# Expert tiles as 32-column strips turned by VectorE instead of TensorE, and landing numbers read before they are needed

## The reference

```
x = layernorm(x + memory_layer(x))        # projections, short convolution, cumulative sums of cos and sin features
flat = x.reshape(4096, 128)
probs = softmax(flat @ router_w.T)        # 8 experts
topk_p, topk_i = top_k(probs, 2); weights = topk_p / sum(topk_p)
out = sum over experts e of square(relu(flat @ w_fc[e].T)) @ w_proj[e].T * combine[:, e]   # w_fc[e]: 512 x 128
out += square(relu(flat @ shared_fc.T)) @ shared_proj.T
x = layernorm(x + out)
```

## Time and profile before

| | us |
|---|---|
| median of 3 runs (lowest, highest) | 480.66 (480.43, 483.86) |
| the profiled execution | 480.25 |
| its span in the profile | 478.4 |
| TensorE busy | 443.9 (93%) |
| VectorE busy | 356.6 (75%) |
| ScalarE busy | 354.9 (74%) |
| GpSimd busy | 318.1 (66%) |

### The profile page before, as it was taken

One profiled execution on the slowest core, in us unless ns is written; L12 is line 12 of the kernel. 1 busy time (PEld: TensorE's weight loads), 2 busy tenths in 40 slices (PEclk: granted clock), 3 DMA queues, 4 the chain that ended last, 5 costly groups with the idle time before them and its releaser, 6 DMA issues.

```text
span 478.4 us, 7874 instructions
## 1 busy us (share of the span) xinstructions
PE 443.9 (93%) x2193; PEld 288.9 (60%) x2193; DVE 356.6 (75%) x870; ACT 354.9 (74%) x557; POOL 318.1 (66%) x294
## 2 busy tenths in 40 slices
PE   8997999999999998877889988999999999999973
PEld 5343444444344333334666766789999999999821
DVE  5889999999999999999888977453333333555465
ACT  3989999999999999952675555556666666666655
POOL 4763788888898989881677667734555545655541
PEclk9998999999999999999999999999999999999999
DMA  8032226673434343200111111142223221222457
GB/s 284 11 93 84 78 73 214 217 245 136 157 136 159 136 157 136 92 1 1 47 45 52 50 41 52 55 111 59 69 68 85 67 65 53 62 70 66 147 176 220
DMA packets 41196, 48.68 MB, mean 102 GB/s; under 512 B 5616, under 2 KB 25266, under 8 KB 41152
## 3 DMA queue, kind: packets, MB, share of 16 engines
q1 hardware_dynamic: 35792, 39.16, 25.0%
q0 software_dynamic: 5216, 8.70, 6.0%
q10 hardware_dynamic: 144, 0.31, 0.3%
HBM read 19.26 MB, written 29.11 MB: 101 GB/s over the span
## 4 chain that ended last, share of the span: by engine, by line
PE 43%; POOL 22%; DVE 17%; issue 8%; ACT 6%; SPq 2%; DMA 2%; POOLq 0%; DVEq 0%; ACTq 0%
POOL memory_feat L505 17%; PE routed_ph L1591 13%; PE routed_po L1606 13%; PE dispatch_spo L1074 3%; PE dispatch_sph L1064 3%; DVE memory_y_raw L788 2%; POOL memory_feat L513 2%; DVE memory_prod L779 2%; POOL memory_prod L528 2%; PE routed_px L1579 2%; PE memory_nsum L630 2%; SPq L1737 1%; DVE memory_feat L779 1%; PE memory_ph L636 1%; DVE dispatch_stats L1319 1%
## 5 line engine op out<-in xcount | busy, mean ns | idle before, releaser
L505 POOL TENSOR_TENSOR memory_feat<-memory_feat,memory_p_tok 128x1024 f32<-128x1024 f32 x64 | 125.9, 2063 | 17.1 <-ACT memory_feat L400 14.2
L630 PE MATMUL memory_nsum<-memory_feat,tri 128*128 128x512 f32 x256 | 116.8, 598 | 6.3 <-ACT memory_last_rows L413 2.4
L1567 POOL DMA_INDIRECT pick_scratch<-routed_ob,routed_xg x71 | 72.1, 1016 | 65.2 <-DVE routed_ob L1689 52.0
L630 PEld LDWEIGHTS memory_nsum<-memory_feat,tri 128*128 128x128 f32 x256 | 47.6, 191 | 64.4 <-issue 54.6
L1274 POOL DMA_INDIRECT table_scratch<-dispatch_xrow,dispatch_slot x64 | 62.3, 973 | 30.3 <-issue 14.4
L1639 ACT ACTIVATE routed_rel<-routed_ph 128x512 f32<-128x512 f32 x71 | 42.3, 597 | 45.0 <-PE routed_ph L1591 45.0
L1689 DVE TENSOR_SCALAR routed_ob<-routed_po,routed_xg 128x128 f32<-128x128 f32 x71 | 22.6, 348 | 67.2 <-PE routed_po L1606 67.1
L1606 PE MATMUL routed_po<-routed_w2c,routed_hid 128*128 128x128 f32 x568 | 71.1, 275 | 0.5 <-ACT routed_hid L1648 0.5
L1591 PE MATMUL routed_ph<-routed_xs,routed_w1c 128*128 128x256 f32 (+1 forms) x368 | 71.2, 337 | 0.0
L779 DVE TENSOR_TENSOR memory_prod<-memory_nsum,memory_query 128x1024 f32<-128x1024 f32 x58 | 68.8, 1216 | 2.0 <-PE memory_nsum L630 1.8
L1606 PEld LDWEIGHTS routed_po<-routed_w2c,routed_hid 128*128 128x128 f32 x568 | 67.0, 192 | 0.8 <-ACT routed_hid L1648 0.7
(11 more groups left out here) (202 smaller groups left out, 695.6 us busy)
## 6 DMA issues: line engine op xcount, KB each, us to landing
table_scratch<-memory_blank SPq DMA_DIRECT2D x68, 260.0 KB, 2.6
dispatch_xrow<-pick_scratch SPq DMA_DIRECT2D x16, 256.0 KB, 3.1
routed_xg<-table_scratch SPq DMA_DIRECT2D x25, 130.0 KB, 2.2
w<-w_up SPq DMA_DIRECT2D x9, 256.0 KB, 2.7
w<-w_down SPq DMA_DIRECT2D x9, 256.0 KB, 3.2
x_tok<-x SPq DMA_DIRECT2D x4, 512.0 KB, 3.7
out<-x_tok SPq DMA_DIRECT2D x7, 256.0 KB, 4.1
routed_xg<-table_scratch SPq DMA_DIRECT2D x21, 65.0 KB, 1.9
```

Of the source, the lines that this page charges most:

```text
L505: nc.gpsimd.tensor_tensor(v, v, pv, ALU.mult).then_inc(wfeat_done, 1)
L630: last = nc.tensor.matmul(nsum[:, o:o + 512], tri[:], feat[:, i % U, h, q * 512:(q + 1) * 512], start=True, stop=True)
L1567: nc.gpsimd.indirect_dma_start(out=pick_dram, in_=ob[:, u, h, :], in_offset=None, out_offset=bass.IndirectOffsetOnAxis(ap=xg[:, t % XU, h, ...
```

## The change

It is made of four edits.

1. A full tile is no longer loaded as 256 rows but as four strips of 32 columns each. A strip goes to 32 partitions of `xb`, cut into 32 x 32 blocks: one DMA with 256 runs of 128 bytes. The two words at the end of each row (place and weight) go to `mark` with a fifth DMA. Tiles 0 and 1 have all four strips begun by SyncE; from tile 2 on SyncE begins two and ScalarE two. Half tiles are loaded as before, into an `xg` that now has one slot of 128 rows for each tile.
2. VectorE turns the 32 x 32 blocks with one instruction for a full tile, from `xb` to `xs`. TensorE's transposes and ScalarE's copies stay for half tiles alone.
3. ScalarE waits at its start of the stage until all 8 groups are in the table, so that it need not know `needs`. Tile 2 is begun ahead of its first relu, then two tiles in each of the steps 0, 1 and 2 (tiles 3 to 8), then tile t+6 in step t, always behind the squares.
4. The numbers of `settle` are read by SyncE in tiles 10 to 17, one group in each, and kept in registers. The two loads of a group now share a semaphore.

```diff
@@ build
-            rou.sync(sp)
-            fin.sync(sp)
+            due = rou.sync(sp)
+            fin.sync(sp, due)
@@ routed
+    ASK_AT = 10
+    SQ = 32
+    STRIPS = D // SQ
+    ALONE = 2
+    LEAD = 6
-        xg = sb("xg", [P, XU, HALVES, RW])
+        xb = sb("xb", [P, XU, ROWS])
+        mark = sb("mark", [P, XU, HALVES, RW - D])
+        xg = sb("xg", [P, XU, RW])
...
+        def by_sync(t):
+            return STRIPS if t < ALONE else STRIPS // 2
...
+        def strip(t, j, rows):
+            return (xb[j * SQ:(j + 1) * SQ, t % XU, :].rearrange("a (i b) -> a i b", b=SQ),
+                    rows[:, j * SQ:(j + 1) * SQ].rearrange("(i a) b -> a i b", a=SQ))
...
+            def full(t):
+                first = sp.value_load(start[0:1, t:t + 1], min_val=0, max_val=TABLE - ROWS)
+                groups = sp.value_load(needs[0:1, t:t + 1], min_val=1, max_val=NG)
+                rows = table[bass.ds(first, ROWS), :]
+                sp.wait_ge(dis.grouped, groups)
+                if not early(t, XU):
+                    sp.wait_ge(blocked, t - XU + 1)
+                for j in range(by_sync(t)):
+                    to, of = strip(t, j, rows)
+                    sp.dma_start(to, of).then_inc(stripped[t % XU], 16)
+                if not early(t, XU):
+                    sp.wait_ge(scattered[t % U], passes(t - XU))
+                sp.dma_start(mark[:, t % XU], rows[:, D:].rearrange("(h p) c -> p h c", p=P)).then_inc(loaded[t % XU], 16)
...
+            def body(t, u):
+                load(t, u)
+                g = t - ASK_AT
+                if g == 0:
+                    sp.wait_ge(dis.settled, 1)
+                if 0 <= g < NG:
+                    due.append([sp.value_load(settle[g:g + 1, n:n + 1], min_val=16, max_val=32 * TILES) for n in range(U)])
...
         def tensor(pe):
             def up(t, u):
-                pe.wait_ge(x_kept, t + 1)
+                if t < FULL:
+                    pe.wait_ge(blocked, t + 1)
+                else:
+                    pe.wait_ge(x_kept, t - FULL + 1)
...
             def front():
-                turn(0, 0)
-                turn(1, 1)
                 up(0, 0)
...
-                if not beyond(t, 2):
-                    turn(t + 2, (u + 2) % U)
+                if not beyond(t, 2) and t + 2 >= FULL:
+                    turn(t + 2)
...
         def scalar(act):
+            def load(t):
+                first = act.value_load(start[0:1, t:t + 1], min_val=0, max_val=TABLE - ROWS)
+                if not early(t, XU):
+                    act.wait_ge(blocked, t - XU + 1)
+                rows = table[bass.ds(first, ROWS), :]
+                for j in range(by_sync(t), STRIPS):
+                    to, of = strip(t, j, rows)
+                    act.dma_start(to, of).then_inc(stripped[t % XU], 16)
+
+            def begun(t):
+                return min(FULL, 2 * t + 5, t + LEAD + 1)
...
             def front():
-                keep_x(0, 0)
-                keep_x(1, 1)
+                act.wait_ge(dis.grouped, NG)
+                for t in range(ALONE, begun(-1)):
+                    load(t)
                 rectified(0, 0)
                 squared(0, 0)
...
                 if not beyond(t, 1):
                     squared(t + 1, (u + 1) % U)
+                for n in range(begun(t - 1), begun(t)):
+                    load(n)
...
         def vector(dve):
+            def turn(t):
+                dve.wait_ge(stripped[t % XU], 16 * STRIPS * (t // XU + 1))
+                if not early(t, 2):
+                    dve.wait_ge(up_done, parts(t - 1))
+                nc.vector.transpose(xs[:, t % 2, :], xb[:, t % XU, :]).then_inc(blocked, 1)
+
+            def front():
+                turn(0)
+                turn(1)
+
             def body(t, u):
                 if not beyond(t, 3):
                     weights(dve, t + 3, (u + 3) % U)
+                if t + 2 < FULL:
+                    turn(t + 2)
                 dve.wait_ge(down_done, t + 1)
+                dve.wait_ge(loaded[t % XU], 16 * (t // XU + 1))
@@ finish
-        def sync(sp):
-            sp.wait_ge(dis.settled, 1)
-
+        def sync(sp, due):
             def load(g):
-                due = [sp.value_load(settle[g:g + 1, u:u + 1], min_val=16, max_val=32 * TILES) for u in range(U)]
                 for u in range(U):
-                    sp.wait_ge(rou.scattered[u], due[u])
+                    sp.wait_ge(rou.scattered[u], due[g][u])
```

More of the change, by code:

```diff
@@ L98, in build @@
         late = Late(nc, c, early.xrow, x_tok)
-        rou = routed(nc, c, dis, ident, w1, w2, expert, start, needs, table, pick_dram)
-        fin = finish(nc, c, late, dis, rou, ident, y_all, eps, warm, settle, pick_dram, out)
+        rou = routed(nc, c, dis, ident, w1, w2, expert, start, needs, settle, table, pick_dram)
+        fin = finish(nc, c, late, rou, ident, y_all, eps, warm, pick_dram, out)
         block = c.enter_context(nc.Block())
@@ L1480, in dispatch, with routed @@
                              grouped=grouped, tabled=tabled, experts_in=experts_in, added=added, settled=settled)
-def routed(nc, outer, dis, ident, w1, w2, expert, start, needs, table, pick_dram):
+def routed(nc, outer, dis, ident, w1, w2, expert, start, needs, settle, table, pick_dram):
     HALVES = ROWS // P
@@ L1508, in routed @@
         px = ps("px", [P, FC * P])
+        stripped = [sem(f"stripped{u}") for u in range(XU)]
         loaded = [sem(f"loaded{u}") for u in range(XU)]
+        blocked = sem("blocked")
         scattered = [sem(f"scattered{u}") for u in range(U)]
@@ L1550, in load @@
                 first = sp.value_load(start[0:1, t:t + 1], min_val=0, max_val=TABLE - ROWS)
[L1551 to L1561 removed]
+                if t == FULL:
+                    sp.wait_ge(dis.grouped, NG)
+                sp.wait_ge(scattered[t % U], passes(t - XU))
+                sp.dma_start(xg[:, row_of(t)], table[bass.ds(first, P), :]).then_inc(loaded[row_of(t)], 16)
+            def load(t, u):
+                if t < FULL:
+                    full(t)
+                else:
+                    half(t)
+            due = []
+            def body(t, u):
[5 more added lines that the diff above has]
+                    due.append([sp.value_load(settle[g:g + 1, n:n + 1], min_val=16, max_val=32 * TILES) for n in range(U)])
+            tiles(lambda: None, body)
+            return due
         def gpsimd(pool):
@@ L1565, in body @@
                 pool.wait_ge(kept, t + 1)
-                for h in range(height(t)):
+                for h, own in enumerate(marks(t)):
                     nc.gpsimd.indirect_dma_start(
                         out=pick_dram, in_=ob[:, u, h, :], in_offset=None,
-                        out_offset=bass.IndirectOffsetOnAxis(ap=xg[:, t % XU, h, D:D + 1].bitcast(U32), axis=0),
+                        out_offset=bass.IndirectOffsetOnAxis(ap=own[:, 0:1].bitcast(U32), axis=0),
                         bounds_check=2 * NTOK - 1, oob_is_err=False).then_inc(scattered[u], 16)
@@ L1573, in tensor @@
         def tensor(pe):
-            def turn(t, u):
-                pe.wait_ge(loaded[t % XU], 16 * (t // XU) + 16)
-                if not early(t, 1):
-                    pe.wait_ge(x_kept, t)
-                for h in range(height(t)):
-                    last = nc.tensor.transpose(px[:, h * P:(h + 1) * P], xg[:, t % XU, h, 0:D], ident[:])
-                last.then_inc(turned, 1)
+            def turn(t):
+                pe.wait_ge(loaded[row_of(t)], 16 * (t // XU) + 16)
+                if t > FULL:
+                    pe.wait_ge(x_kept, t - FULL)
+                nc.tensor.transpose(px[:, 0:P], xg[:, row_of(t), 0:D], ident[:]).then_inc(turned, 1)
             def up(t, u):
                 s = u % 2
-                pe.wait_ge(x_kept, t + 1)
+                if t < FULL:
+                    pe.wait_ge(blocked, t + 1)
+                else:
+                    pe.wait_ge(x_kept, t - FULL + 1)
                 pe.wait_ge(w_ready, t + 1)
@@ L1712, in finish @@
         both = [c.enter_context(nc.psum_tensor(f"finish_both{g}", [P, GT * D], F32)) for g in range(NG)]
-        picked = [[sem(f"picked{g}_{r}") for r in range(2)] for g in range(NG)]
+        picked = [sem(f"picked{g}") for g in range(NG)]
         both_done = sem("both_done")
@@ L1822, in gpsimd @@
             for n, g in enumerate(BY_POOL):
-                for r in range(2):
-                    pool.wait_ge(picked[g][r], 16)
+                pool.wait_ge(picked[g], 32)
                 v = slice(g * GT, (g + 1) * GT)
@@ L1831, in add_up @@
             def add_up():
-                for r in range(2):
-                    dve.wait_ge(picked[0][r], 16)
+                dve.wait_ge(picked[0], 32)
                 v = slice(0, GT)
```

49 lines of the change are left out of this document (21 added, 28 removed).

## The result

The changed kernel takes 483.28 us (median of 20 runs, 481.63 to 486.08) beside 480.64 us for the kernel before (20 runs, 479.11 to 485.23). The ratio is 1.0044, 95% interval 1.0027 to 1.0061: slower by 2.1 us by the ratio (the two medians lie 2.6 us apart), which is inside the 1% called "within". The forecast was 475.2 us, faster by 5.5. The profiled execution took 484.4 us with a span of 482.6, that is 1.1 us over its median and 4.2 us over the profiled one before.

What follows compares the result with a forecast made beforehand. TensorE was taken to bound full and half tiles, SyncE's register reads the end. The terms -4.9 + 1.9 + 0.5 - 3.0 = -5.5 us took 480.66 to 475.2; own range 472.5 to 477, overall 472.0 to 481.0.

Steps and rivals of the forecast that it cites:

- SyncE's lag: Tiles 10 to 17: SyncE falls 11 us behind against a 13 us lead; charged at nothing, upper end 2 us.
- the last stage: End: with early reads, ScalarE and VectorE set about 1.95 us a group; -3.0 us, ends -1 and -4.5.
- transposes off TensorE: Full tiles: 23 steps lose 0.215 us each once TensorE no longer transposes; -4.9 us.
- start of up(0): First up of the full tiles waits for VectorE's first turn, beginning near 318.8; +1.9 us.
- rival B: Start: TensorE's 3.0 us pause drops the granted clock to 0.50, costing 1.7 us, 476.9 in all; chance 0.10.
- ScalarE issuing: Steps 0 to 2, two tiles each: ScalarE 1.1 us over, slack absorbing most; +0.5 us, ends 0 and 1.5.
- rival C: Full steps: ScalarE's issuing doesn't overlap its squares, a tile costs 4.2 us against 3.52; slower, 489.5; chance 0.13.
- rule of overlap: Full tiles: ScalarE's issuing runs beside its squares, as VectorE's register read did; 2.9 us a tile instead of 4.2.
- DMA engines: Full tiles: at 34 ns a piece, 2.7 us plus 0.4 of scatters fit inside 3.52; engines bound from 39 ns.
- rival D: Full tiles: short runs choke the DMA engines; at 45 ns each, 4.0 us a tile, 486.7, slower; chance 0.06.
- rival E: Last stage: ScalarE's best pace, some 1.75 us a group, 0.8 us more gain, 473.8 in all; chance 0.08.
- rival A: Last stage: SyncE's reads didn't pace it; real pace 2.5 us a group, gain there 0.8, 477.4; chance 0.13.

Runs made afterwards that it cites:

- after: The changed kernel, with all four edits made to the kernel before: 483.28 us, ratio 1.0044 to the kernel before.
- no_pool: The changed kernel with GpSimd's adds for groups 2 to 6 given to TensorE: 481.6 us, ratio 1.0014 to the kernel before.
- reads_spread: The changed kernel with SyncE's 32 reads of settle one to a tile, tiles 9 to 40: 480.97 us, ratio 0.9998 to the kernel before.
- shift_ts: The changed kernel with each shift made by four tensor_scalar instead of one scalar_tensor_tensor: 480.61 us, ratio 0.9987 to the kernel before.
- spread_ts3: The changed kernel with reads one to a tile and the first three shifts by four tensor_scalar each: 476.33 us, ratio 0.9896 to the kernel before.
- reads_back: The changed kernel with the reads of settle back in the last stage, strips kept: 479.97 us, ratio 0.9978 to the kernel before.
- warm: The changed kernel with 7 unused 128x512 matmuls ahead of the first up: 482.63 us, ratio 1.0019 to the kernel before.
- warm3: The changed kernel with 3 unused 128x512 matmuls ahead of the first up: 484.25 us, ratio 1.0072 to the kernel before.
- turns_first: The changed kernel with earlier turns of tiles 0 and 1, SyncE alone loading three tiles, ScalarE's wait behind its first squares: 484.57 us, ratio 1.0094.
- spread_turns: The changed kernel with reads one to a tile plus the edit of turns_first: 476.42 us, ratio 0.9907 to the kernel before.
- spread_turns_ts3: The changed kernel with spread reads, the edit of turns_first and the first three shifts by tensor_scalar: 473.26 us, ratio 0.9830 to the kernel before.
- reads_alone: The kernel before with only the reads of settle moved to tiles 10 to 17, no strips: 481.95 us, ratio 1.0015 to the kernel before.
- alone_ts3: The kernel before with reads in tiles 10 to 17 and the first three shifts by tensor_scalar, no strips: 478.21 us, ratio 0.9942.

## Why the prediction was wrong, point by point

The forecast was -5.5 us and the ratio gives +2.1. Three steps of the working failed: SyncE's lag, put at nothing, cost 3.6 us; the last stage, put at -3.0, gave -0.4, because VectorE's shift waited for GpSimd's adds; and the clock, put at nothing in the sum, cost 2.0. Between the two profiled executions the terms are:

| step | foretold | measured | from |
|---|---|---|---|
| end of dispatch, ahead of the change | 0 | +1.4 | 317.19 against 315.80 |
| transposes off TensorE | -4.9 | -5.1 | 23 x 0.22, full steps of 3.51 us against 3.73 |
| start of up(0) | +1.9 | +1.8 | 3.02 us from the end of dispatch, against 1.18 with two turns inside |
| clock | 0 (rival B +1.7) | +2.0 | 5.42 against 3.46 us |
| ScalarE issuing, first steps | +0.5 | +0.9 | below |
| SyncE's lag | 0 (end: +2) | +3.6 | the turn of tile 21 |
| last stage | -3.0 | -0.4 | below |

They add up to +4.2, and the spans differ by 4.2. The first term has nothing to do with the change: dispatch ended anywhere from 315.4 to 318.6 us in the fourteen profiles. Without it 2.8 are left, beside 2.1 by the ratio.

**Transposes and turn: right.** The turn cost 0.44 us (0.4 taken) and lay beside TensorE's work. The step without transposes is 0.22 us shorter, so the 0.215 taken was a little low.

**Start: right.** up(0) was released by VectorE's turn, as foretold; it began at 320.21 instead of near 318.8 because dispatch itself ended 1.4 us later. The "3.0 us" of rival B is the pause that was measured.

**Clock: this was rival B, given 0.10.** The earlier trace rows had shown it after a pause of 3.23 us, and the prediction counted on a pause of 3.0 being short enough; it was not. With this pause (2.98 to 3.02 us) sixteen ups took 5.4 us in the profiles of after, no_pool, reads_spread, shift_ts and spread_ts3, but 3.7 at a clock of 1.00 in that of reads_back. So after a pause of this length it fell in five of six profiled executions, and the same start can differ by 2 us. Why reads_back kept its clock isn't shown. In the five profiles in which the pause was filled or shortened to at most 0.41 us (warm, warm3, turns_first, spread_turns, spread_turns_ts3) it never fell there.

**ScalarE issuing: right in kind, sized low, and rival C dead.** In the three steps with two tiles' loads each, ScalarE's step was 4.36 us (in the chain, relus at 329.96, 334.28 and 338.68). TensorE's up(2), down(4) and up(6) show what of it came through:

```profile
327.24 1.89 PE L1643 MATMUL routed_ph<-routed_xs,routed_w1c 128*128 128x256 f32 x8
...
340.36 2.05 PE L1658 MATMUL routed_po<-routed_w2c,routed_hid 128*128 128x128 f32 x16 [0.62 <-ACT routed_hid L1709]
342.24 1.89 PE L1643 MATMUL routed_ph<-routed_xs,routed_w1c 128*128 128x256 f32 x8
```

Four tiles took 15.00 us instead of 4 x 3.51, so 0.9 was lost, nearly twice the charge and inside its ends. With one tile a step nothing was. The rule of overlap, read off VectorE's sequencer in the earlier trace rows, holds for ScalarE.

**DMA engines: right, rival D dead.** From 345 to 365 us queue 10, which has ScalarE's strips, had 3,315 packets at 15.2% of 16 engines: 0.152 x 16 x 20 us / 3,315 = 15 ns each, where 34 was the bound taken. Here belongs the rule of the Trainium skill weighed in the prediction ("DMA: Bandwidth & Descriptors", Specifications): a transfer of under 512 B leaves line rate. The trace agrees on the direction, since 128 bytes in 15 ns are fewer bytes per ns than 520 in 34. But a piece cost less, not more, so the doubling that gave 529 us wasn't there: the three queues together took 0.37 of the engines' time, and TensorE stood still for none of it in this stretch.

```profile
q10 hardware_dynamic: 3315, 0.40, 15.2%
q1 hardware_dynamic: 2991, 0.27, 11.7%
q0 software_dynamic: 384, 0.79, 10.3%
```

**SyncE's lag: the first step that failed.** The prediction set a lag of 11 us against a lead of 13 and called it narrow. The lag was (5.14 - 3.51) x 8 = 13.0 us: a tile with reads costs 5.14, not 4.9. (From 331 on a tile without reads cost 2.78, where 2.6 was taken; the four reads are the other 2.36.) An issue of tile 18's strips that took 1.7 us added 1.4. The lead was worse: SyncE wasn't held back by the scatter of tile t-9, as assumed. It issued a tile each 3.0 us from 321 to 342 (seven tiles, 321.19 to 342.27) without any wait, still building up a lead: it had begun tile 0 only at 310.75. At tile 10 its strips went out at 342.27, and the turn of tile 10 stood at 354.42; less issue (0.8) and landing (1.7) that is a lead of 9.6 (the landing is an estimate from tiles 17 and 18, whose turns began 1.7 us after the end of SyncE's issue). So 13.0 + 1.4 - 9.6 = 4.8 us, the wait of 4.76 at the turn of tile 18. A turn stands 1.6 us ahead of its up in the undisturbed steps (344.33 to 345.92), which absorbed some of it; 3.6 came through. By the ratios of the timed runs spreading the reads gave back 2.2, with the late scatter of 0.8 coming in. The mistake was to take the steady state's lead for a queue that starts with none.

**Last stage: the second step that failed.** The pace was mended and more: 1.56 us a group, where 1.95 was taken (and 1.75 by rival E). From ScalarE's first normalisation to the end of the span it took 16.7 us (465.94 to 482.6) instead of 21.9 (456.51 to 478.4), 5.2 less. But that first one came 4.9 us later, counted from the last `routed_ob` (457.16 after, 452.60 before): together -0.4. The step "next is the pair of ScalarE and VectorE" was wrong: next was VectorE's shift against GpSimd's adds. The rows to see it by were in the profile before, unread:

```profile
461.58 0.55 DVE L1860 SCALAR_TENSOR_TENSOR finish_shift<-finish_mv,finish_rstd 128x4 f32<-128x4 f32 x1
464.73 0.70 DVE L1860 SCALAR_TENSOR_TENSOR finish_shift<-finish_mv,finish_rstd 128x4 f32<-128x4 f32 x1
...
471.09 0.16 DVE L1860 SCALAR_TENSOR_TENSOR finish_shift<-finish_mv,finish_rstd 128x4 f32<-128x4 f32 x1
```
```profile
465.47 0.81 ACT L1803 ACTIVATE x_tok<-finish_both,finish_shift,finish_rstd 128x128 f32<-128x128 f32 x2 [1.61 <-DVE finish_shift L1860]
```
```profile
460.86 1.26 POOL L1826 TENSOR_TENSOR dispatch_xrow<-dispatch_xrow 128x512 f32<-128x512 f32 x1 [1.89 <-DMA dispatch_xrow<-pick_scratch]
464.15 1.26 POOL L1826 TENSOR_TENSOR dispatch_xrow<-dispatch_xrow 128x512 f32<-128x512 f32 x1 [2.04 <-DMA dispatch_xrow<-pick_scratch]
```

The same instruction takes 0.16 us when GpSimd is idle, and up to 0.70 when an add runs: 461.58 + 0.55 = 462.13 beside 460.86 + 1.26 = 462.12, and 465.43 beside 465.41. It ended when the add did. The 0.94 us that ScalarE waited ahead of group 2, which the earlier trace rows shows and rival A weighed, ended with that shift, and so did 1.61 us ahead of the next group (465.47). SyncE's slow reads kept the adds 3 us apart, so it never met more than one. The early loads put all five in a row, 6.18 us long, with the first shift, on which all of ScalarE's work waits, inside. The Trainium skill has this rule ("SBUF — State Buffer", Who interferes with whom): a VectorE instruction with two inputs in SBUF contends with a GpSimd instruction that reads SBUF, through a pair of ports that one of them holds to its end. The trace agrees on who contends: scalar_tensor_tensor was held for 5.16 us, four tensor_scalar with a pointer scalar took 0.57 us. On how long, the section speaks of the whole of one instruction, and here the loser waited for all five.

Two sums of the prediction are off without changing the account: rival E takes 0.6 us of issuing away where 0.5 was charged, and rival C's 0.65 a tile is 0.68 by its own numbers (4.2 - 3.52).

## What to carry to other kernels

Work that is moved into a queue has to be weighed against that queue's lead at that moment, not against its lead in the steady state; spread one to a step, the same 32 reads delayed no strip. When a slow issuer is sped up, everything that it had kept apart comes at once: list what will then run side by side, and look for an instruction whose time already varies with its neighbour's (0.16 to 0.70 us here). And an improvement upstream of a fixed pace downstream (warm3, turns_first) shows no gain until that pace is mended, so such edits have to be tried together.

## What the runs showed of the hardware that was not expected

- VectorE's scalar_tensor_tensor of 4 elements per partition took 5.14 to 5.16 us beside five back-to-back GpSimd adds of 128x512 (6.15 to 6.18 us), in seven profiles; without the adds 0.16. In shift_ts batch-norm statistics from PSUM (four in 0.88 us) and tensor_scalar (four in 0.57 us) took as long beside the adds as after them.
- In six profiles with early loads (reads_spread, reads_alone, warm, warm3, spread_ts3, alone_ts3) a scatter of 64 KB, begun between 446 and 448.4 us, took 6.5 to 7.3 us to land instead of 2.4. The DMA engines moved 291 to 355 GB/s from 446 to 454 us there, most of it pick loads. That these delay the scatter isn't shown: in turns_first (354 GB/s) and spread_turns_ts3 (368) nothing waited for one, nor in after, no_pool, shift_ts and spread_turns.
- Of SyncE's strip issues (0.32 us median) single ones took 1.2 to 1.8 us. What they met isn't shown.
- VectorE turns 128x256 f32 in 32 x 32 blocks in 0.44 us, about what its copy of 128x512 takes.
